# Gate products of a recurrent kernel computed as two column halves in PSUM banks of their own

## What is computed

```python
h = cond                                    # layer 0: a plain RNN
h = tanh(h @ Whh + x_t @ Wx + b);  x = x + hs
weights = softmax(cond . x / sqrt(512), over the batch of 2);  x = x + x * weights
x = x + tanh(x @ W_ih.T + cond @ W_hh.T + b_ih + b_hh)
# layer 3: a GRU over the 2048 steps
z = sigmoid([x_t, h] @ Wz + bz);  r = sigmoid([x_t, h] @ Wr + br)
c = tanh([x_t, r * h] @ Wh + bh)
h_new = (1 - z) * h + z * c                 # the output of the step
h = tanh(h_new @ Wp + bp) if (t + 1) % 4 == 0 and t < 2047 else h_new
```

## Time and profile before

| | us |
|---|---|
| median of 3 runs | 8802.99 (8791.31 to 8805.06) |
| profiled execution, its own time | 8793.52 |
| its span, first to last instruction | 8791.7 |
| PE busy | 8661.0 (99%) |
| PE weight loads busy (overlap PE) | 6952.4 (79%) |
| DVE busy | 5044.1 (57%) |
| ACT busy | 4687.6 (53%) |
| POOL busy | 997.6 (11%) |
| granted TensorE clock, mean | 0.997 |

### The profile page before, as it was taken

How to read it: one execution, slowest core, us unless ns; L and a number is a source line. 1 busy time by engine, 2 the same in 40 slices (tenths; PEclk the granted TensorE clock), 3 DMA queues, 4 the chain that set the end, 5 groups by cost and what they waited for, 6 DMA issues and landing times.

```text
span 8791.7 us, 669547 instructions
## 1 busy us (share of the span) xinstructions
PE 8661.0 (99%) x291880; PEld 6952.4 (79%) x291880; DVE 5044.1 (57%) x26506; ACT 4687.6 (53%) x26367; POOL 997.6 (11%) x4362
## 2 busy tenths in 40 slices
PE   8999999999999999999999999999999999999998
PEld 6778777877787778778787778777877787778776
DVE  3555555555555555555555555555555555555555
ACT  3555555555555555555555555555555555555554
POOL 1111111111111111111111111111111111111110
PEclk8999999999999999999999999999999999999999
DMA  1000000000000000000000000000000000000000
GB/s 67 11 12 10 10 11 12 10 10 10 13 10 10 10 13 10 10 10 12 11 10 10 11 12 10 10 11 12 10 10 10 13 10 10 10 13 10 10 11 11
DMA packets 133369, 105.97 MB, mean 12 GB/s; under 512 B 14976, under 2 KB 132096, under 8 KB 132096
## 3 DMA queue, kind: packets, MB, share of 16 engines
q1 hardware_dynamic: 133248, 104.20, 3.9%
HBM read 62.20 MB, written 41.94 MB: 12 GB/s over the span
## 4 chain that ended last, share of the span: by engine, by line
PE 98%; issue 1%; DVE 0%; ACT 0%; DMA 0%; SPq 0%; POOL 0%; DVEq 0%; ACTq 0%
PE ps_r L398 23%; PE ps_c L398 22%; PE ps_l L398 21%; PE ps_z L398 20%; PE ps_p L398 6%; PE ps_mid L385 5%; PE ps_proj L385 2%; DVE l_T L536 0%; DVE ps_p L539 0%; PE ps_logit L434 0%; DMA rnn_h<-w_rnn_h 0%; DVE h_ring L647 0%; ACT l_ring L685 0%; ACT ps_l L659 0%; ACT scan_add L724 0%
## 5 line engine op out<-in xcount | busy, mean ns | idle before, releaser
L398 PE MATMUL ps_l<-rnn_h,l_ring 128*2 128x128 f32 x65536 | 2179.3, 274 | 26.8 <-ACT ps_l L659 26.8
L398 PE MATMUL ps_c<-c_h,rh 128*2 128x128 f32 x65536 | 2165.0, 272 | 6.3 <-DVE rh L602 2.4
L398 PEld LDWEIGHTS ps_c<-c_h,rh 128*2 128x2 f32 x65536 | 1397.2, 84 | 543.8 <-DVE rh L602 376.3
L398 PEld LDWEIGHTS ps_l<-rnn_h,l_ring 128*2 128x2 f32 x65536 | 1723.8, 85 | 112.2 <-ACT ps_l L659 36.9
L398 PE MATMUL ps_r<-r_h,h_ring 128*2 128x128 f32 x49152 | 1671.7, 272 | 18.7 <-DVE h_ring L647 18.7
L398 PE MATMUL ps_z<-z_h,h_ring 128*2 128x128 f32 x49152 | 1623.8, 273 | 0.2 <-issue 0.2
L398 PEld LDWEIGHTS ps_r<-r_h,h_ring 128*2 128x2 f32 x49152 | 994.9, 83 | 542.4 <-DVE h_ring L647 478.9
L398 PEld LDWEIGHTS ps_z<-z_h,h_ring 128*2 128x2 f32 x49152 | 1291.6, 85 | 50.4 <-issue 0.6
L539 DVE STREAM_TRANSPOSE ps_p<-ps_r 128x32 f32<-128x32 f32 x2048 | 473.4, 231 | 1329.0 <-PE ps_r L398 1329.0
L539 DVE STREAM_TRANSPOSE ps_p<-ps_c 128x32 f32<-128x32 f32 x2048 | 473.6, 231 | 1128.3 <-PE ps_c L398 1128.3
L319 POOL TENSOR_TENSOR y<-x,h_ring 128x8 f32<-128x8 f32 x2048 | 347.6, 201 | 4951.9 <-DVE h_ring L647 4951.9
(11 more groups left out here) (85 smaller groups left out, 9399.0 us busy)
## 6 DMA issues: line engine op xcount, KB each, us to landing
gates_spill<-gates_rows SPq DMA_DIRECT2D x128, 192.0 KB, 1.9
gates_seeds<-gates_spill SPq DMA_DIRECT2D x512, 48.0 KB
x_next<-xT SPq DMA_DIRECT2D x128, 64.0 KB, 1.7
x_mid<-xT SPq DMA_DIRECT2D x128, 64.0 KB, 1.7
rnn_spill<-rnn_rows SPq DMA_DIRECT2D x128, 64.0 KB, 1.5
rnn_seeds<-rnn_spill SPq DMA_DIRECT2D x512, 16.0 KB
y_out<-y SPq DMA_DIRECT2D x128, 64.0 KB, 1.6
rcz_x<-w_rc_x SPq DMA_DIRECT2D x1, 2048.0 KB, 9.0
```

The costliest lines, as they stand in the source:

```text
L398: last = nc.tensor.matmul(psum[QUAD * j:QUAD * j + B, 0:P], stationary(k), w[:, k, P * j:P * (j + 1)], start=False, stop=(k == KT - 1), sk ...
```

## The change

r, c and p are computed as two halves n of 64 columns each (W = 64; two k tiles of the result each, KH = 2). Each half has its own bank: `ps_r` and `ps_c` become pairs of banks, p moves into c's pair at other columns, and the softmax logits move into the bank of `ps_proj`. z and l keep their 128 columns. The 16 calls of 128 columns become 32 calls of 64. PE does three parts ((k, n) = (0,0), (0,1), (1,0); for p (0,0), (1,0)) on the low half of the state, waits for the high half, finishes n = 0, signals it, and then finishes n = 1. DVE waits for each half by itself and transposes 64 columns within the bank. ACT seeds a pair of banks with one copy; after every fourth step c's seed comes behind p's tanh and seed. FRONT is gone.

```diff
-        r_T, c_T, p_T = ([bank[:, P:2 * P].rearrange("p (k r) -> p k r", k=KT)[:, k, :] for bank, k in
-                          ((front, slice(0, FRONT)), (others, slice(FRONT, KT)))]
-                         for front, others in ((ps_p, ps_r), (ps_p, ps_c), (ps_r, ps_p)))
+        ps_z, ps_l, ps_mid, ps_proj = (bank(n) for n in ("ps_z", "ps_l", "ps_mid", "ps_proj"))
+        ps_r, ps_c = (ctx.enter_context(nc.psum_tensor(n, [P, 2, 512], fp32)) for n in ("ps_r", "ps_c"))
+        R_AT, C_AT, P_AT = 0, 0, W
+        r_T, c_T, p_T = ([pair[:, n, at:at + W].rearrange("p (k r) -> p k r", k=KH) for n in range(2)]
+                         for pair, at in ((ps_r, W), (ps_c, 2 * W), (ps_c, 3 * W)))
...
+            def halved_product(pair, at, stationary, w, ready, count, done, inc, early=((0, 0), (0, 1), (1, 0))):
+                def part(k, n):
+                    for j in range(NJ):
+                        last = nc.tensor.matmul(pair[QUAD * j:QUAD * j + B, n, at:at + W], stationary(k), w[:, k, P * j + W * n:P * j + W * (n + 1)],
+                                                start=False, stop=(k == KT - 1), skip_group_check=True)
+                    return last
+                if ready is not None:
+                    pe.wait_ge(ready[0], count)
+                for k, n in early:
+                    part(k, n)
+                if ready is not None:
+                    pe.wait_ge(ready[1], count)
+                for n in range(2):
+                    for k in range(KT):
+                        if (k, n) not in early:
+                            last = part(k, n)
+                    last.then_inc(done[n], inc)
...
-                        seeded_product(ps_r, state, r_h, ready, count).then_inc(r_product, 1)
+                        halved_product(ps_r, R_AT, state, r_h, ready, count, r_product, 1)
...
-                        seeded_product(ps_c, lambda k: rh[:, k, :], c_h, rh_ready, t_gru + u + 1).then_inc(c_product, 1)
+                        halved_product(ps_c, C_AT, lambda k: rh[:, k, :], c_h, rh_ready, t_gru + u + 1, c_product, 1)
...
+            def transpose_piece(n, product, pair, at, pieces, T_done, count, inc=1):
+                dve.wait_ge(product[n], count)
+                nc.vector.transpose(pieces[n].rearrange("p k r -> p (k r)"), pair[:, n, at:at + W]).then_inc(T_done[n], inc)
...
-                        if u % PROP == 0:
-                            dve.wait_ge(p_seeded, t + PROP)
-                        dve.wait_ge(r_product, t + 1)
-                        pieces_transposed(r_T, ps_r, r_T_done)
+                        for n in range(2):
+                            transpose_piece(n, r_product, ps_r, R_AT, r_T, r_T_done, t + 1)
...
+            def seed_pair(pair, at, rows):
+                return nc.scalar.activation(pair[:, :, at:at + W], rows.rearrange("p (h n) -> p h n", h=2), ACT.Copy)
```

More of the change, by code:

```diff
@@ L63, in piece_sems @@
         def piece_sems(name):
-            return [sem(name + "_front"), sem(name + "_others")]
+            return [sem(name + "_low"), sem(name + "_high")]
         rnn_x = sb("rnn_x", KT, D)
@@ L387, in product, with seeded_product @@
                 return last
-            def seeded_product(psum, stationary, w, ready, count):
+            def seeded_product(psum, stationary, w):
                 for k in range(KT):
-                    if ready is not None and k in (0, FRONT):
-                        pe.wait_ge(ready[k // FRONT], count)
                     for j in range(NJ):
@@ L420, in _ @@
             pe.wait_ge(seeds_clear, 3)
-            for psum in (ps_l, ps_z, ps_p, ps_r, ps_c):
+            for psum in (ps_l, ps_z, ps_r[:, 0, :], ps_r[:, 1, :], ps_c[:, 0, :], ps_c[:, 1, :]):
                 open_bank(psum).then_inc(banks_open, 1)
@@ L433, in softmax_logits @@
                 for j in range(NJ):
-                    last = nc.tensor.matmul(ps_logit[QUAD * j:QUAD * (j + 1), 0:ROWS], ones[:, :], qx_sum[:, :], start=True, stop=True)
+                    last = nc.tensor.matmul(ps_proj[QUAD * j:QUAD * (j + 1), logits_at], ones[:, :], qx_sum[:, :], start=True, stop=True)
                 last.then_inc(logit_product, 1)
@@ L651, in iteration @@
                     if u % PROP == PROP - 1 and gru and not last_step(i, u):
-                        dve.wait_ge(p_product, t + 1)
-                        pieces_transposed(p_T, ps_p, p_T_done, PROP)
+                        for n in range(2):
+                            transpose_piece(n, p_product, ps_c, P_AT, p_T, p_T_done, t + 1, PROP)
             all_iterations(dve, iteration)
@@ L672, in seed_gate @@
                 after(act, T_done, STEPS * (i - LAG) + u)
-                seed(psum, gates_seeds[:, u, gate, :]).then_inc(seeded, 1)
+                if gate == 2:
+                    seed(psum, gates_seeds[:, u, gate, :]).then_inc(seeded, 1)
+                else:
+                    seed_pair(psum, R_AT if gate == 0 else C_AT, gates_seeds[:, u, gate, :]).then_inc(seeded, 1)
             def seed_next_gate(i, u, gate, psum, T_done, seeded):
@@ L711, in iteration @@
                     if gru:
-                        for n, (k, _) in enumerate(PIECES):
+                        for n, k in enumerate(PIECES):
                             act.wait_ge(r_T_done[n], t + 1)
```

53 lines of the change are left out of this document (25 added, 28 removed).

## The result

| | before | after |
|---|---|---|
| median, us | 8799.64 (8791.31 to 8805.06, 4 runs) | 16352.32 (16332.91 to 16357.32, 4 runs) |
| ratio | 1 | **1.858** [1.855, 1.861] |
| span of the profiled execution | 8791.7 | 16331.1 |
| granted clock, mean | 0.997 | 0.888 |

A forecast was written before the change was run, and what follows sets the result against it. PE (TensorE), busy 99%, was taken as the bound; from 8793.5 us, - 410 + 74 + 60 + 100 + 1624 + 630 gave 10870 us, case range 10000 to 11700, 8-in-10 range 8450 to 13000 us.

The forecast's parts named there:

- the two waits per step: In PE's loop, c waits for rh and the next r for h, losing 0.14 to 0.38 us a step.
- The cost of a halved product: On PE, smaller matmuls add 0.016 us (between 0 and 0.08) to each halved product: +74 us.
- Rival D: A PE round gets no shorter than at width 128, halved products take 1.74 us: 12400 us without fetches; chance 0.04.
- The code: PE's loop body grows from 6 to 8 blocks, one is fetched ahead, and no more than 8 are held.
- The straight-line chunks: In chunks outside the loop, PE waits for code at 3.5 us a block: +100 us (0 to 150).
- The step that failed: At PE's jumps back, the overwritten first block is fetched again: 13.2 us a chunk, +1624 us.
- rival C: The oldest block is always replaced, so PE fetches every block again in every group: about 14100 us; chance 0.14.
- Rival A: PE's loop code stays resident, only - 410 + 74 + 60 + 100 count: 8620 us (8450 to 8770); chance 0.21.
- The clock term: PE's granted clock halves behind three of four stalls a chunk: +630 us (0 to 840).
- The - 410 us: In the loop, halves remove all PE waits for DVE and ACT, 0.20 us a step over 2048 steps.
- The + 60 us at the branches: Around a group's four branches, PE's queue holds records worth half the time under p: +60 us (0 to 150).

The follow-up runs named there:

- e3: Changed kernel with all halves, but PE's inner loop shortened to two steps run twice (some 1140 instructions, 5 blocks): 9009.82 us, 1.024.
- e2: Kernel before, nothing halved, with 29 two-column matmuls added after each z product in the loop (1777 instructions, 7 blocks): 10910.03 us, 1.244.
- e12: Form of e9 with r halved in all four loop steps and c in three (some 1770 instructions, 7 blocks): 10202.36 us, 1.160.
- e11: Changed kernel with half of z's and l's columns left out, same instructions (1889, 8 blocks): 16084.14 us, 1.827.
- e4: Kernel before with whole products and PE's inner loop shortened to two steps run twice (some 820 instructions, 4 blocks): 8914.15 us, 1.013.
- e10: Form of e9 with c halved in all four loop steps and the next x's projection moved out of the inner loop (6 blocks): 8628.48 us, 0.980.
- e7: Form of e6 with r halved in the second to fourth step of each loop group (some 1510 instructions, 6 blocks): 9016.39 us, 1.025.
- e6: Kernel before in the changed bank layout, no product halved, transposes in pieces of 64 and 64 columns (6 blocks): 9278.75 us, 1.055.
- e9: Kernel before with c halved in three loop steps; whole products waited for once, transposed in 32 and 96 columns (6 blocks): 8685.42 us, 0.987.

## Why the prediction was wrong, and where it was right

**Read right.** PE as the bound, the two waits per step and what removes them: where no code is waited for, c follows z and r follows l after 0.87 us, with r and c halved (e3). The cost of a halved product: l comes 0.89 us behind a halved c, where 0.87 is a whole one, 0.02 us more; 0.016 was taken. Rival D, a round no shorter than at width 128, falls with it, as the earlier trace rows had said. The code: 6 blocks and 8, one fetched ahead, no more than 8 held. The straight-line chunks: + 100 us forecast, + 116 measured.

**The step that failed** is the one that said what happens once nine blocks share eight places: "entering the eighth block fetches the ninth over the first, and the jump back finds its target gone". That is right as far as it goes. The sum then stopped there, with one fetch at each jump, as if the first block's return hurt no other. It throws out the next one that is needed, and so on round the body. This was rival C, at 0.14, with the remark that nothing in the trace tells the two ways apart; nothing there did, and the chance of a case that costs three times as much should have decided the upper end of the range. The range left C out. e2 and e12 show the round by itself: one block too many once a chunk brings nine packets in every chunk of e12 and in 91 of 117 of e2. The way that the forecast had taken does occur, in e2's other 26 chunks with two packets, but in no chunk of the changed kernel, each of which has 37 in the middle of the loop.

**C's own size was off too**, 14100 us (its own terms, on top of A's 8620, give 14030) against 16352. It had 8 fetches a group at 3.5 us, 28 us. There are 9.25 packets a group: the block behind the body is fetched anew in every group too, and one more comes with the chunk's head. But one packet of each group comes close behind another, so that these add little: a group is 8.25 distances of 3.83 us and one of 0.50. What was too small is above all the time of a fetch: the prediction had found 3.4 to 4.1 us and taken 3.5. That the fetches and not PE's work set the 3.83 us is what e11 shows.

**The clock term**, + 630 us for a halved clock behind each stall: the clock did fall, to 0.89 in the mean of the loop, but behind fetches that set the pace it can't cost much: e11 has nearly the same low clock (0.86) and 1132 us less busy time on PE, and is 268 us faster.

**The - 410 us** were too large for what the halves give. Where the code fits, e3 has 0.11 us a step less than e4, and only in steps that no jump ends; e10's four halved c products give 0.084 us a step. Two parts were not in the working: r's chain has a fixed length from r's start, so that what is saved within r is waited for at c, and a jump between l and r costs as much as the wait it hides. The + 60 us at the branches were 0.19 us at each mid product and 0.39 at each chunk's end in e3, 118 us over the loop. Rival A's 8620 us, the change with its code resident, is therefore out of reach by the halves as written. e3 stands 96 us above e4, for the straight-line chunks; by this reckoning resident code would have brought about no change, not a gain, though no run has the changed loop at its own length with its code resident.

**What stays open.** By what rule places are refilled. By age or in a fixed turn would give the same packets in the changed kernel and in e12, and neither gives e2's chunks with two. Also open is r's own share in halves at the length of before, since e7 carries the second wait's cost.

## What to carry to other kernels

Before a change multiplies the instructions of a loop on TensorE, count them: a call in fp32 is four, and the loop with its outer head and the block behind it has to stay within eight blocks of 256. One block too many is mostly not paid once but by fetching the whole loop, here 3.8 us for each block, and where that comes in every pass the work done in it hardly matters any more. If an idea costs code, spend the room where a wait ends (here c in all four steps, with one projection moved out of the body, - 2.0%), and leave straight-line code as it was.

## What the runs showed of the hardware beyond what was expected

- Fetches of code that follow one another keep a pace of their own: 3.83 us from one to the next in the changed kernel, 3.78 with 31 added matmuls, 3.75 with a part of the work left out, though a group there has 3.4 us less to do (means of the distances over 2 us; with the close ones at the jumps 3.47, 3.51 and 3.42).
- Where chunk head, body and the block behind are nine blocks, a chunk fetches either nine of them or two, in one and the same kernel (e2: 91 and 26 of 117 chunks).
- A second semaphore wait ahead of an instruction on DVE goes with a start 0.10 us later (1.22 against 1.12 us after the product's start, e6). e6 moved tiles between banks as well, so the wait as its cause is inferred, though e9 without it has its c 0.11 us sooner behind z (0.97 against 1.08 us, of which 0.03 belong to the narrower first piece).
- Two-column matmuls with their weight loads cost 0.14 us for 13 calls and 0.42 us for 29, 11 to 14 ns a call of two matmuls, while the columns of a tile are spread over four column tiles.
